# Splitting one statistics step, moving a shared-expert unit ahead of the experts, and reordering the last sums of a gated block

## What is computed

```
x = x + tanh(g_xattn) * conv_attention(ctx, ctx, layernorm(x), ssm_kernel, D)   # 16 heads of 8
h = rmsnorm(layernorm(x)) * w_norm                                             # 2048 tokens
w, sel = top_k(softmax(h @ w_router), 4)                                       # 32 experts, 4 per token
buf[e, pos] = h[token]                       # at most 128 tokens per expert, in order of arrival
y[e] = (silu(buf[e] @ w_gate[e]) * (buf[e] @ w_up[e])) @ w_down[e]
shared = sigmoid(h @ w_shared_gate) * ((silu(h @ sw_gate) * (h @ sw_up)) @ sw_down)
x = x + tanh(g_ffn) * (layernorm(x) + sum over the token's experts of w * y + shared)
```

## Time and profile before

| | |
|---|---|
| median of three executions | 332.99 us (330.82 to 333.48) |
| profiled execution, its own time | 335.25 us |
| its span | 333.5 us |
| mean granted TensorE clock | 0.972 |
| PE busy | 300.6 us, 90% |
| weight load on PE | 249.6 us, 75% |
| DVE busy | 214.5 us, 64% |
| POOL busy | 200.1 us, 60% |
| ACT busy | 123.9 us, 37% |
| chain that ended last | PE 52%, DVE 16%, SP's queue 13%, DMA 7% |

### The profile page before, as it was taken

One profiled execution on the slowest core, in us unless ns is written; L12 is line 12 of the kernel. 1 busy time (PEld: TensorE's weight loads), 2 busy tenths in 40 slices (PEclk: granted clock), 3 DMA queues, 4 the chain that ended last, 5 costly groups with the idle time before them and its releaser, 6 DMA issues.

```text
span 333.5 us, 5037 instructions
## 1 busy us (share of the span) xinstructions
PE 300.6 (90%) x1548; PEld 249.6 (75%) x1548; DVE 214.5 (64%) x518; ACT 123.9 (37%) x352; POOL 200.1 (60%) x233
## 2 busy tenths in 40 slices
PE   5899868965999989999699999499999999998993
PEld 4798768954998778998478777277777777876782
DVE  2689996764859997679854711034454454368696
ACT  3248344952277401449026801134334334231000
POOL 3998996437688957784476777116665663342300
PEclk9999988997999999999899999789999999999998
DMA  5997999995011111021077730519999999977287
GB/s 186 291 316 221 292 268 385 386 279 174 36 71 47 62 53 53 36 68 38 18 204 227 227 87 1 142 58 227 218 249 226 251 233 235 301 179 238 31 267 239
DMA packets 52970, 59.40 MB, mean 178 GB/s; under 512 B 6570, under 2 KB 48550, under 8 KB 52944
## 3 DMA queue, kind: packets, MB, share of 16 engines
q1 hardware_dynamic: 42272, 47.24, 47.2%
q0 software_dynamic: 7392, 8.69, 13.3%
q10 hardware_dynamic: 3280, 3.15, 2.9%
HBM read 36.83 MB, written 26.94 MB: 191 GB/s over the span
## 4 chain that ended last, share of the span: by engine, by line
PE 52%; DVE 16%; SPq 13%; DMA 7%; issue 5%; POOL 5%; DVEq 0%; ACT 0%
PE Y L1268 12%; PE pg L1101 6%; POOL dispatched L415 5%; PE pu L1101 5%; SPq L322 4%; PE pd L1287 4%; PE Y L1287 4%; SPq L312 4%; SPq L318 3%; PE Y L1089 3%; PE Y L1090 3%; PE Y L1091 3%; DVE arena L802 3%; PE Y L1259 3%; DMA arena<-in_ctx_dram 2%
## 5 line engine op out<-in xcount | busy, mean ns | idle before, releaser
L415 POOL DMA_INDIRECT dispatched<-rows,dsu x64 | 64.0, 1000 | 32.0 <-issue 24.6
L494 POOL DMA_INDIRECT expert_sum<-arena,ide x30 | 47.6, 1588 | 57.0 <-DVE arena L984 31.2
L405 POOL TENSOR_TENSOR arena<-arena 128x256 f32<-128x256 f32 x96 | 57.4, 634 | 4.0 <-ACT arena L508 3.6
L970 DVE TENSOR_TENSOR arena<-arena,Y 128x176 f32<-128x176 f32 x32 | 10.8, 337 | 47.5 <-ACT arena L708 42.6
L1089 PE MATMUL Y<-arena 128*128 128x192 f32 x128 | 33.9, 348 | 5.9 <-DVE arena L794 5.3
L802 DVE TENSOR_REDUCE arena<-arena 128x128 f32<-128x1024 f32 x32 | 38.7, 1211 | 0.2
L1091 PE MATMUL Y<-arena 128*128 128x192 f32 x128 | 33.1, 342 | 0.0
L1090 PE MATMUL Y<-arena 128*128 128x192 f32 x128 | 33.1, 342 | 0.0
L701 ACT ACTIVATE arena<-Y,wn 128x128 f32<-128x128 f32 x64 | 20.0, 363 | 33.6 <-PE Y L1259 33.4
L1089 PEld LDWEIGHTS Y<-arena 128*128 128x128 f32 x128 | 22.9, 201 | 9.9 <-issue 7.2
L1268 PE MATMUL Y<-arena 128*128 128x352 f32 x88 | 29.7, 460 | 0.0
(11 more groups left out here) (215 smaller groups left out, 670.9 us busy)
## 6 DMA issues: line engine op xcount, KB each, us to landing
expert_sum<-zrow SPq DMA_DIRECT2D x3, 2176.0 KB, 17.5
dispatched<-zrow SPq DMA_DIRECT2D x1, 4624.0 KB, 21.7
arena<-dispatched SPq DMA_DIRECT2D x32, 144.5 KB, 3.8
arena<-in_L_ffn_w_gate_dram SPq DMA_DIRECT2D x22, 176.0 KB, 2.8
arena<-in_L_ffn_w_up_dram SPq DMA_DIRECT2D x22, 176.0 KB, 3.9
arena<-in_L_ffn_w_down_dram SPq DMA_DIRECT2D x22, 176.0 KB
first_slots<-expert_sum SPq DMA_DIRECT2D x4, 512.0 KB, 6.2
arena_sum<-expert_sum SPq DMA_DIRECT2D x4, 512.0 KB, 6.3
```

What stands on the lines that cost most here:

```text
L405: ins = pool.tensor_tensor(o[:, :, blk], i0, i1, ALU.mult)
L415: pool.indirect_dma_start(buf, bass.IndirectOffsetOnAxis(ap=dsu[:, t % 2, j:j + 1], axis=0), rows[:, t % 2, j // K, :], None, bounds_check ...
L494: pool.indirect_dma_start(accs[a], bass.IndirectOffsetOnAxis(ap=ide[:, e % NO:e % NO + 1], axis=0), ye[:, e % NO, :], None, compute_op=ALU ...
```

## The change

It does six things.
1. ACT's statistics of group 3 are cut in two. The sums come at p = 6 and the squares at p = 7 of the walk over group 1, behind the `silu` of the unit there; before, both came at p = 5. POOL's `query_pow(3)` moves from p = 6 to p = 7.
2. DVE's `token_slots` is cut into `token_ranks` and the rest. For the tokens of group 0 the rest moves from the end of group 1's walk behind the first step of group 2's.
3. POOL issues `send(2, 5)` before `xn_low(3, ...)` instead of behind it.
4. Unit 32 moves from behind expert 25 to before the experts, right behind unit 31, with the banks pg and pu. Unit 33 moves from behind expert 26 to behind expert 25; nothing follows expert 26 any more.
5. SOLO becomes 28: experts 27 and 25 and 23 go to sum 1, and 24, 26, 28, 29 to sum 0. Sum 1 is loaded at once, in four pieces, when 28 experts are done and its additions have landed. DVE adds its first two pieces behind `use(36)` after expert 29.
6. DVE adds the first four pairs of sum 0 between `y_low(30)` and `e_yout(31)`. Behind that, it adds pair i + 4 of sum 0 and then the result of `own` for pair i.

```
 NPRE, NW, NX, NO = 5, 16, 8, 8
-CLOSE, SOLO, OWN = 23, 26, 2
+CLOSE, SOLO, OWN = 23, 28, 2
 ADDED = E - OWN
+AHEAD = 4
 OHN = 512
 ONEHOT_AT = 28
-LOAD2_AT, LOAD1_AT = 23, 26
-ADD2_AT, ADD1_AT = 25, 28
+LOAD2_AT, LOAD1_AT = 23, 28
+ADD2_AT, ADD1_AT = 25, 29
...
 LATE = 18
-TWICE = range(20, 32)
+TWICE, LAST_BANKS = range(20, 33), 31
 WARM = 6
-UNITS_EXPERT = range(32, 40)
-UNIT_STEP = {25: (32,), 26: (33,), 27: (34,), 29: (35, 36, 37), 30: (38, 39)}
+UNITS_EXPERT = range(33, 40)
+UNIT_STEP = {25: (33,), 27: (34,), 29: (35, 36, 37), 30: (38, 39)}
...
         def in_y(n):
-            return n in TWICE and (NJ * (n // UNITS) + n % UNITS) % 2 == 0
+            return n in TWICE and n < LAST_BANKS and (NJ * (n // UNITS) + n % UNITS) % 2 == 0
...
         def gate_out(n):
-            return pd[:] if n == TWICE[-1] else Y[:, 0] if in_y(n) else pg[:]
+            return pd[:] if n == LAST_BANKS else Y[:, 0] if in_y(n) else pg[:]
...
         def up_out(n):
-            return pm[:] if n == TWICE[-1] else Y[:, 1] if in_y(n) else pu[:]
+            return pm[:] if n == LAST_BANKS else Y[:, 1] if in_y(n) else pu[:]
...
                     sp.wait_ge(add_sem[a], all_added(a))
-                if a:
-                    sp.wait_ge(s["e_y"], (0, LOAD1_AT, LOAD2_AT)[a] + i)
+                if a == 2:
+                    sp.wait_ge(s["e_y"], LOAD2_AT + i)
+                elif a == 1 and i == 0:
+                    sp.wait_ge(s["e_y"], LOAD1_AT)
                 elif i == 0:
...
                     load_sum(2, e - LOAD2_AT)
-                if LOAD1_AT <= e < LOAD1_AT + G:
-                    load_sum(1, e - LOAD1_AT)
+                if e == LOAD1_AT:
+                    for i in range(G):
+                        load_sum(1, i)
             for i in range(2 * G):
...
                         token_pow(t)
-                    if p == 6 and g + 2 < G:
-                        query_pow(g + 2)
                     if p in (4, 5):
...
                     if p == 7:
+                        if g + 2 < G:
+                            query_pow(g + 2)
                         send(t, 0)
...
             token_pow(G - 1)
-            for i in range(3, 5):
+            for i in range(3, 6):
                 send(G - 2, i)
...
             pool.wait_ge(s["lg_ready"], G)
-            for i in range(5, 8):
+            for i in range(6, 8):
                 send(G - 2, i)
...
+            def q_squares(g):
                 for b in range(GB):
...
             q_stats(2)
+            q_squares(2)
             act_e.wait_ge(s["sw_in"], 64)
...
                             query(g + 1, p + 1)
-                    if p == 7 and g + 2 < G:
-                        q_coef(g + 2)
-                        query(g + 2, 0)
                     if p == 2:
...
                             xn_high(t, c)
+                    if p == 6 and g + 2 < G:
+                        q_stats(g + 2)
+                    if p == 7 and g + 2 < G:
+                        q_squares(g + 2)
+                        q_coef(g + 2)
+                        query(g + 2, 0)
                     if p == 4:
...
                             exps(t)
-                        if g + 2 < G:
-                            q_stats(g + 2)
...
-            def token_slots(t):
+            def token_ranks(t):
                 dve.wait_ge(s["rank_done"], t + 1)
...
+            def token_slots(t):
                 link(dve.scalar_tensor_tensor(out=rk[:], in0=ge[:], scalar=FAR, in1=rk[:], op0=ALU.mult, op1=ALU.add))
...
                     if p == 6 + (g == 1):
-                        token_slots(t)
+                        token_ranks(t)
+                        if g > 1:
+                            token_slots(t)
+                    if (g, p) == (2, 0):
+                        token_slots(0)
...
             token_gates(t)
+            token_ranks(t)
             token_slots(t)
...
+            two = {}
+            def add_first(i):
+                dve.wait_ge(fin_sem[0][i], 16)
+                dve.wait_ge(s["down_used"], downs[0])
+                two[i] = mark(dve.tensor_tensor(x_pair(i), x_pair(i), sums[0][:, 2 * i:2 * i + 2], ALU.add))
...
                     y_low(e - 1)
+                    for i in range(AHEAD):
+                        add_first(i)
                 e_yout(e)
-                if e == ADD1_AT + 2:
+                if e == ADD1_AT + 1:
                     add_sum(1, G - 2)
...
                     downs[0] += m % UNITS >= NJ
+                    if m == 36:
+                        add_sum(1, 0)
+                        add_sum(1, 1)
                 if ADD2_AT <= e < ADD2_AT + G:
...
                         dve.sem_inc(s["sum2_used"], 1)
-                if ADD1_AT <= e < ADD1_AT + 2:
-                    add_sum(1, e - ADD1_AT)
                 for k in range(4 * OWN):
...
             dve.wait_ge(s["down_used"], GB * G)
-            two = {}
...
             for i in range(2 * G):
-                dve.wait_ge(fin_sem[0][i], 16)
-                two[i] = mark(dve.tensor_tensor(x_pair(i), x_pair(i), sums[0][:, 2 * i:2 * i + 2], ALU.add))
-                if i:
-                    add_own(i - 1)
-            add_own(2 * G - 1)
+                if i + AHEAD < 2 * G:
+                    add_first(i + AHEAD)
+                add_own(i)
...
                     pe.wait_ge(s["y_used"], NP_ * G)
-                elif n == TWICE[-1]:
+                elif n == LAST_BANKS:
                     pe.wait_ge(s["rank_used"], G)
+                elif n > LAST_BANKS and n in TWICE:
+                    pe.wait_ge(s["down_used"], GB * gs)
                 elif n in TWICE:
...
                     pe.wait_ge(s["silu_done"], k)
-                    if n == UNITS_EXPERT[0]:
-                        pe.wait_ge(s["down_used"], GB * gs)
                 split_product(gate_out(n), gs, j * P if j < NF else 2 * NF * P).then_inc(s["gate_done"], 1)
...
                 if j < NF:
-                    if n == TWICE[-1]:
+                    if n == LAST_BANKS:
                         pe.wait_ge(s["rank_used"], G)
+                    elif n > LAST_BANKS and n in TWICE:
+                        pe.wait_ge(s["down_used"], GB * gs)
                     elif n in TWICE:
...
                 if e == 0:
-                    pe.wait_ge(s["act_ready"], NJ * (UNITS_EXPERT[0] // UNITS) + UNITS_EXPERT[0] % UNITS - 1)
+                    pe.wait_ge(s["act_ready"], NJ * (LAST_BANKS // UNITS) + LAST_BANKS % UNITS)
                 if e:
...
                 if e == 0:
-                    pe.wait_ge(s["act_ready"], NJ * (UNITS_EXPERT[0] // UNITS) + UNITS_EXPERT[0] % UNITS)
+                    pe.wait_ge(s["act_ready"], NJ * (LAST_BANKS // UNITS) + LAST_BANKS % UNITS + 1)
                 else:
...
```

## The result

| | before | after |
|---|---|---|
| median, 16 runs each | 333.52 us | 328.73 us |
| lowest and highest | 330.82, 335.81 | 326.65, 330.87 |
| profiled execution, its own time | 335.25 us | 327.85 us |
| its span | 333.5 us | 326.1 us |
| mean granted clock | 0.972 | 0.976 |

The ratio of after to before is 0.9864, with a 95% interval of 0.9837 to 0.9892: 4.5 us faster, between 3.6 and 5.4. The forecast was 6.4 us and 326.6, in a range of 323.9 to 330.8. By the ratio 1.9 us of the forecast gain did not come, by the second 0.9. The time alone decides little: 328.73 is nearer to the 329.2 and 329.5 of rivals C and D than to 326.6. The ratios and medians of the experiments leave out executions that took over 1.5% longer than the fastest of their kernel.

What follows compares the result with a forecast made beforehand. Bounds in turn: the last contexts' load, POOL's indirect DMAs, PE with a low clock at first, then DVE and the DRAM sums. Gains 0 + 0.6 + 2.6 + 3.2 = 6.4 us from 332.99 give 326.6, range 323.9 to 330.8.

Steps and rivals of the forecast that it cites:

- Rival C: Opening of the experts: TensorE's clock falls to 0.50 anyway; gain only 3.8, 329.2 us; chance 0.14.
- Rival D: First chain or dispatch's index cast loses one or two POOL operations, clock gain partly lost: 329.5 us; chance 0.08.
- Part 1: First chain, items 1 and 2: work ends sooner but waits for the same contexts' load; gain 0, bounds 1.2 either way.
- Part 2: Dispatch, item 3: send(3, 0) waits for the slots and starts sooner; gain 0.6 us.
- Part 3: Unit 32 ahead of the experts, item 4: TensorE no longer idles, clock stays at 1.00; gain 2.6 us, bounds 0 and 3.1.
- Part 4: The end, items 5 and 6: earlier loads of sum 0, fewer additions after y_low(31); gain 3.2 us, bounds 0 and 4.2.
- rival B: The end: sum 0's loads go out no sooner, at 317; 3.2 us gained, 329.8 us; chance 0.13.
- The stores follow each addition as before: The end: each store was to follow its addition as in the kernel before; no extra time counted.
- 7.5: The end: us after y_low(31), being TensorE's 6.8 to its last matmul plus one addition of 0.68.
- Rival E: The end: DVE's wait on add_first idles TensorE, its clock falls, 7.8 us more; slower, 337.6 us; chance 0.05.
- the rule on two SBUF inputs: Dispatch: two-input DVE and GpSimd instructions exclude each other; DVE could lose 1.26 us, making it a loss of 0.5.
- The signs of being wrong: Clock 0.50 at 213, a DVE wait on DMA at L1013 or L1054 over 2 us, or group 3's start moving from 79.

Runs made afterwards that it cites:

- no_first_chain: The changed kernel with items 1 and 2 undone (ACT's statistics and DVE's token_slots uncut): 328.75 us, 0.9827 of the kernel before.
- keep_warm: The changed kernel with useless TensorE transposes in two idle places, ahead of the last group's contexts and the ranks' last one-hot transposes: 326.56 us, 0.9769 of before.
- dispatch_only: The kernel before with item 3 alone (send(2, 5) ahead of the last xn_low): 332.83 us, 0.9964 of before.
- busy_pe: The kernel before with 26 useless transposes of the identity on TensorE after unit 31: 331.35 us, 0.9909 of before.
- after_again: The whole change measured once more, unaltered (the "second" measurement of the result): 328.94 us, 0.9837 of the kernel before.
- no_ahead: The changed kernel with item 6 alone undone, all eight pairs of sum 0 behind y_low(31): 328.67 us, 0.9813 of the kernel before.
- unit_only: The kernel before with item 4 alone (unit 32 ahead of the experts, unit 33 behind expert 25): 330.98 us, 0.9892 of before.
- no_tail: The changed kernel with items 5 and 6 undone, so the old ending: 332.23 us, 0.9927 of the kernel before.
- tail_only: The kernel before with items 5 and 6 alone: 334.33 us, 0.9994 of before.
- no_unit: The changed kernel with item 4 undone (unit 32 back behind expert 25, unit 33 behind 26): 334.26 us, 1.0018 of the kernel before.

## Why the prediction was right, and where its sizes were off

- **Part 1, 0 us.** Right, with its cover as named: the contexts' load. Not foreseen: the idle time gathers in one piece of 5.2 us. The median shows no price for it (no_first_chain).
- **Part 2, 0.6 us.** The local step is right: `send(3, 0)` starts 0.93 us behind the cast instead of 1.67, 0.74 sooner, and POOL waits for DVE. But the cast itself came 0.49 later after TensorE's resumption (186.33 - 77.34 = 108.99, before 187.65 - 79.15 = 108.50), which leaves 0.25 in this profile. In keep_warm, with the clock high, that cast comes 106.33 us after TensorE's resumption. The local step is seen once more in dispatch_only, where TensorE's wait for the experts' rows is 0.78 shorter.
- **Part 3, 2.6 us.** Right in mechanism, and shown: busy_pe gets 2.39 of the 2.46 us of the opening with useless work, at 2.6 forecast. Rival C falls in every kernel in which TensorE stayed busy almost until the experts: the clock was at 1.00. The free place of unit 32 is right too: it ends 0.12 us ahead of the first transpose.
- **Part 4, 3.2 us.** Mis-sized. Sum 0's loads came 5.7 us sooner, with 5.6 forecast, so rival B falls. `y_low(31)` gained 1.39 us in one profile and 0.45 in the other (0.5 forecast), in which DVE waited 2.3 us for sum 1's pieces instead of 1.3; the last stretch gained 2.00 and 0.98 (2.3 forecast); behind it the stores cost 0.51 and gave back 0.14. The ending is thus worth 2.9 us in the first profile and 1.6 in the second. Three steps failed. "The stores follow each addition as before": at 0.6 us per 256 KB they do not. And in the first profile DVE and not TensorE is the last: its additions run without a gap from 316.17, and the last one starts 0.5 us after TensorE's last matmul has ended (321.37 + 0.28), so the stretch from the end of `y_low(31)` is 7.8 us, twelve additions and a first wait of 0.47. Where TensorE is the last, the forecast of "7.5" took TensorE at full rate through its last 6.8 us: in after_again and keep_warm the 1.96 us of idleness that the four early additions cause were followed by a fall of the clock, which costs 1.0. Rival E had that mechanism and set it only beyond a `y_low(31)` at 323, at a price of 7.8; here the fall cost 1.0, as the clock was back after some 3 us, and it does not wait for that point.
- **The attribution within part 4** was wrong as well: item 6 was credited with the shorter last stretch, and no_ahead is as fast without it.
- **The terms are not independent.** I let the 2.74 us of TensorE pass through to DVE and then filled them with four additions. That sum needs item 5: without it DVE holds the last unit's `act` behind sum 1's pieces (unit_only, no_tail). Item 4 alone gives 3.6, items 5 and 6 alone 0, together with the rest 4.5 to 5.5, each within some 1.4 us; the waits in the profiles say more here than the times.
- **Rival D**, meetings on DVE and POOL, did not show in the change itself; it showed as soon as additions were given to POOL. The cast of group 1 in rows 4, which the prediction took as agreeing with the rule on two SBUF inputs, has a single input, so that row does not test the rule as it was put there.
- **The signs of being wrong.** The clock was not at 0.50 at 213. But group 3's start did move, from 79.15 to 77.34, with a load issued 1.71 us sooner (chance, above), and in after_again DVE waited 2.26 us for a piece of sum 1, over the 2 us named. That wait belongs to part 4's missing gain.

What stays open: why the same idle time of 1.96 us is followed by a fall of the clock in two profiles and not in two others (after, no_first_chain), nor after 2.08 us in tail_only, and what sets the load's issue between 69.2 and 72.1.

## What to carry to other kernels

Idle time of TensorE just ahead of its critical work has two prices, the wait and the clock behind it; filling it is worth trying by itself, with useless work if there is no useful work (2.4 us from two fills here, 3.0 from one). Moving an addition across the point on which the last engine waits gains nothing if the same engine stands on both sides: move the work to an engine that is done, and count what the two cost each other. When two edits of one change touch the same queue, measure each alone and each left out: the ending showed nothing alone and 2.1 to 3.0 us beside item 4. And compare two profiles stretch by stretch from a common event, since here 1.7 us of the difference lay ahead of a load whose time follows no edit.

## Not expected of the hardware

- After 1.96 or 2.51 us of idleness TensorE resumed at full rate and its clock fell to 0.50 only 0.7 to 1.4 us into its work (316.96 in after_again; 323.96 in no_unit, where it was back at full rate by 327.5). In unit_only such a fall after 2.01 us of idleness made twelve matmuls take 4.69 us instead of 3.05.
- Four DVE comparisons of 128x512 with a single tensor input took 3.23 us beside POOL's additions and 1.67 without.
- When the last five of eight stores of 256 KB were released 0.6 us apart, the DMA engines moved about 340 GB/s, and the span ended 3.26 us after the last addition, against 2.75 where all but the last were 1.2 us apart.
